# A two-hop graph attention kernel on one core: a drain behind every single matmul and transpose of TensorE in both hops, in place of one behind each group

## What is computed

```python
def _agg(ent, rel, head, tail, etype, fc_w, fc_b):
    a_input = concatenate([ent[head], ent[tail]], axis=-1)
    e_input = sum((a_input @ fc_w.T + fc_b) * rel[etype], axis=-1)
    e = leaky_relu(e_input, negative_slope=0.2)
    m = segment_max(e, head)
    exp_e = exp(e - m[head])
    alpha = exp_e / segment_sum(exp_e, head)[head]
    return segment_sum(ent[tail] * alpha[:, None], head) + ent
for _ in range(2):
    ent = _agg(ent, rel, head, tail, etype, fc_w, fc_b)
    ent = ent / max(norm(ent), 1e-12)
return layernorm(x + ent)
```

## Time and profile before

| what | value |
|---|---|
| median of three runs | 2866.54 us |
| the profiled execution | 2870.03 us |
| its span, first to last instruction | 2867.7 us |
| mean granted TensorE clock (1 is full) | 0.561 |
| TensorE matmul busy | 1218.3 us (42%) |
| TensorE weight load busy | 818.2 us (29%) |
| VectorE busy | 1848.4 us (64%) |
| ScalarE busy | 866.2 us (30%) |
| GpSimd busy | 1805.7 us (63%) |
| bytes moved by DMA | 255.95 MB |

### The profile page before, as it was taken

How to read it: one execution, slowest core, us unless ns; L and a number is a source line. 1 busy time by engine, 2 the same in 40 slices (tenths; PEclk the granted TensorE clock), 3 DMA queues, 4 the chain that set the end, 5 groups by cost and what they waited for, 6 DMA issues and landing times. The chain is left out here.

```text
span 2867.7 us, 22941 instructions
## 1 busy us (share of the span) xinstructions
PE 1218.3 (42%) x4597; PEld 818.2 (29%) x4597; DVE 1848.4 (64%) x3677; ACT 866.2 (30%) x1585; POOL 1805.7 (63%) x1607
## 2 busy tenths in 40 slices
PE   4688801354423544245433534444344345343300
PEld 4577701122211222123212423232223223222200
DVE  6867864286562865546655559877667667766753
ACT  2232304375453754445631212111111111111111
POOL 1000047377774777757777238877777787777776
PEclk9555555555555555555555556665655555566555
DMA  2333333254432444335433133222222222222210
GB/s 68 89 109 103 104 70 84 52 147 131 126 91 71 130 132 131 86 95 150 122 87 114 51 112 89 82 85 79 61 83 87 72 66 84 86 58 66 60 44 13
DMA packets 91815, 255.95 MB, mean 89 GB/s; under 512 B 31782, under 2 KB 39047, under 8 KB 91771
## 3 DMA queue, kind: packets, MB, share of 16 engines
q1 hardware_dynamic: 41403, 183.66, 20.8%
q0 software_dynamic: 50368, 71.78, 11.4%
HBM read 157.76 MB, written 102.23 MB: 91 GB/s over the span
## 5 line engine op out<-in xcount | busy, mean ns | idle before, releaser
L572 POOL DMA_INDIRECT area<-rows,gi x1176 | 1330.2, 1131 | 487.4 <-issue 367.7
L620 POOL DMA_INDIRECT out<-area,place x392 | 459.3, 1172 | 119.5 <-issue 119.5
L765 PE MATMUL psR<-area,row_t 128*98 128x512 f16 (+1 forms) x896 | 302.7, 504 | 454.3 <-DVE area L1191 335.9
L748 PE MATMUL psR<-area 128*128 128x392 f16 x392 | 198.5, 506 | 445.2 <-issue 406.3
L670 PE MATMUL psP<-V,vT 65*125 65x40 f32 (+1 forms) x1586 | 323.4, 393 | 86.1 <-issue 56.6
L670 PEld LDWEIGHTS psP<-V,vT 65*125 65x125 f32 (+1 forms) x1586 | 316.0, 310 | 104.7 <-issue 62.4
L765 PEld LDWEIGHTS psR<-area,row_t 128*98 128x98 f16 x896 | 141.5, 173 | 610.4 <-DVE area L1191 351.9
L908 ACT ACTIVATE area<-area 128x896 f32<-128x896 f32 x84 | 79.8, 950 | 586.2 <-DVE area L1270 433.6
L872 ACT ACTIVATE area<-iota_h,half_hi 128x392 f16<-128x392 f16 x392 | 238.9, 609 | 16.8 <-issue 15.4
L1269 DVE TENSOR_TENSOR area<-SM,rd 128x896 f32<-128x896 f32 x56 | 93.6, 1671 | 206.6 <-DMA out<-area,place 205.4
L774 PE MATMUL psT<-ones,area 98*128 98x1 f32 x700 | 152.6, 352 | 173.5 <-DVE area L1191 131.1
(11 more groups left out here) (269 smaller groups left out, 2296.4 us busy)
## 6 DMA issues: line engine op xcount, KB each, us to landing
rows<-area SPq DMA_DIRECT2D x50, 787.5 KB
area<-tail_digits SPq DMA_DIRECT2D x28, 896.0 KB
rows<-area SPq DMA_DIRECT2D x28, 735.0 KB
area<-rows SPq DMA_DIRECT2D x28, 735.0 KB
area<-rows SPq DMA_DIRECT2D x25, 787.5 KB
area<-rows,gi POOLq DMA_INDIRECT x1176
head_xs<-area SPq DMA_DIRECT2D x28, 448.0 KB
area<-head_xs SPq DMA_DIRECT2D x28, 448.0 KB
```

The source lines that it names most:

```text
L572: pool.indirect_dma_start(out=to[:, b, k, 0:tab.shape[1]], out_offset=None, in_=tab, in_offset=bass.IndirectOffsetOnAxis(ap=gi[:, b, n, k: ...
L620: pool.indirect_dma_start(out=out, out_offset=bass.IndirectOffsetOnAxis(ap=place[:, b, k:k + 1].bitcast(U32), axis=0), in_=rowO[:, b, k, 0 ...
L748: te.matmul(psC, sign_lo[:, (s0 + k) % KS, :], sign_hi[:, (s0 + k) % KS, :], start=static and t0 + k == 0, stop=True, skip_group_check=True)
L765: te.matmul(psR[g % 2][0:HH, 0:w], row_t[:, n, c, :], hot_lo[:, c, 4 * g * P:4 * g * P + w], start=c == 0 and n == 0, stop=c == HB - 1 and ...
```

## The change

A drain stands behind every transpose in `transposes`, every matmul in `products` when it is called from `project`, and every matmul of both kinds in `look`; only the last one of a group carries the increment. `products` of the nodes, ahead of the hops, keeps one drain (`single=False`). In `count` the drain was already behind each matmul; there only the way in which the increment is written changes. In the built program of before the increments were already part of the drains (in the body of the first loop of TensorE there are 42 drains and 4 separate semaphore instructions); in the changed one that body has 88 drains for its 88 matmuls and transposes, and the same 4.

```diff
@@ transposes
                     for k in range(t, min(t + KT, n)):
                         te.transpose(psT[0:w, t // KT, (k - t) * P:(k - t) * P + parts], row(k),
-                                            ident[0:parts, 0:parts])
-                    pe.drain()
-                    pe.sem_inc(tr, 1)
+                                     ident[0:parts, 0:parts])
+                        last = pe.drain()
+                    last.then_inc(tr, 1)
-            def products(n, parts, w, pr):
+            def products(n, parts, w, pr, single=True):
                 half = -(-n // 2)
                 for k in range(n):
                     te.matmul(psP[0:parts, k // half, (k % half) * w:(k % half + 1) * w],
-                                     vT[:, k * P:k * P + parts], V[:, 0:w], start=True, stop=True)
-                pe.drain()
-                pe.sem_inc(pr, 1)
+                              vT[:, k * P:k * P + parts], V[:, 0:w], start=True, stop=True)
+                    if single or k == n - 1:
+                        last = pe.drain()
+                last.then_inc(pr, 1)
@@ node_products
-                products(KN, PN, 2 * R, s_npr)
+                products(KN, PN, 2 * R, s_npr, single=False)
@@ count
-                    pe.drain()
-                    pe.sem_inc(s_cnt, 1)
+                    pe.drain().then_inc(s_cnt, 1)
@@ look
                             te.matmul(psR[g % 2][0:HH, 0:w], row_t[:, n, c, :], hot_lo[:, c, 4 * g * P:4 * g * P + w],
                                              start=c == 0 and n == 0, stop=c == HB - 1 and n == 1)
-                    pe.drain()
-                    pe.sem_inc(s_look, 1)
+                            last = pe.drain()
+                    last.then_inc(s_look, 1)
...
                 for k in range(K):
                     te.matmul(sums[:, k:k + 1], chosen[0:HH, k * P:(k + 1) * P], ones[0:HH, 0:1], start=True, stop=True)
-                pe.drain()
-                pe.sem_inc(s_sum, 1)
+                    last = pe.drain()
+                last.then_inc(s_sum, 1)
```

## The result

Four executions of the changed kernel took 3015.66 to 3046.08 us, median 3029.66; the kernel before beside it 2869.96 us (median of four). The ratio is 1.0555, 95% interval 1.0493 to 1.0618. The forecast was 2990 us (2915 to 3075). The profiled execution took 3033.28 us, its span 3031.0, against 2870.03 and 2867.7: 163.3 us more span.

The account below looks back on a forecast made before the run. GpSimd was taken to bound both hops, with TensorE nearly the chain in the passage between them. Added to the profiled 2870.03 us, 70 (passage) + 48 (first hop's slow stretches) + 2 (second hop) = 120 us gave 2990 us, range 2915 to 3075.

Parts of the forecast that it names:

- The sum of 120 us: Whole kernel: 70 us between the hops, 48 in the first hop, 2 in the second, giving 2990 us; chance 52%.
- The price of one: On TensorE, a drained matmul costs its columns and 0.39 us, taken from the sign matmuls' 0.72 us pitch.
- The passage, +70: Between the hops, TensorE is nearly the chain: 60.85 us become 130.4, 70 us more, with ends of 54 and 80.
- The first hop in its normal course, hidden: First hop: TensorE's chunk grows from 22.6 to 33.0 us, still under GpSimd's 40.3, so nothing is paid.
- The slow stretches of the first hop, +48: Four times in the first hop each instruction is slow; added drains cost 12 us each time, 48 us (0 to 92).
- The second hop, hidden: +2: Second hop: TensorE's chunk of 38.0 us stays under GpSimd's 41.7; only the smaller lead at its start costs 2 us.
- Only the passage pays: Rival, 21%: the first hop's slow stretches last no longer, only the piece between the hops costs: +72, 2942 us.
- The second hop becomes TensorE's: Rival, 14%: drains add 7.4 us to each second-hop chunk, TensorE needs 45.4 us against 41.7: 92 us, 3082 in all.
- Faster: Rival, 7%: drains prevent long bursts, so first-hop waits mostly go: 90 us gained against 72 paid, 2852 us.
- No difference: Rival, 6%: drains cost nothing where TensorE has idle time, or are not carried out singly: 2870 us.
- What would show it: Signs in the changed profile: pitches 0.82, 0.66, 0.86 us; L601 near 150 us; L1143 up some 40; L1269 smaller.

Follow-up runs that it names:

- e5_passage_only: Single drains only in projections 24 to 27, looks 0 to 2 and the seam's, against the kernel before: 2970.66 us beside 2925.87, ratio 1.0197.
- r3_after_third: The unaltered changed kernel run a third time, against the kernel before on another chip without slow stretches: 2822.73 us beside 2766.49, ratio 1.0186.
- e9_inc_third: The changed kernel with its 1792 added drains replaced by increments of an unread semaphore, against the kernel before: 2895.73 us beside 2871.14, ratio 1.0139.

## Why the prediction was right, and where its steps were not

- **The sum of 120 us** stands against 163 measured, inside the range. Its passage was named rightly, its second hop wasn't. That it came out inside owes something to luck: the passage was 13 us too large, the second hop 83 too small, GpSimd's busy time fell by 23 us of which the sum says nothing, and the first hop's size came out right for a wrong reason. It also took a chip with slow stretches; on one without them the same change costs 56 us.
- **The price of one** was put too high. Measured in the changed kernel: transposes 7.63/14 = 0.55 us (0.66 forecast), fp32 products 10.10/14 = 0.72 (0.86), 512 columns 11.75/16 = 0.73 (0.82), 256 columns 0.52 (0.61), sums 0.65 (0.83). The row that I took it from, the sign matmul at 0.72 us, has something in its 0.21 us that the others have not: in the trace, though not in the timeline view, a register instruction of the ring starts 0.084 us ahead of its weights (900.709 and 900.793, behind the stretch of the earlier trace rows). Without it 392 columns cost 0.635 us, and 120 more 0.1: 0.735, as measured. The price of a drained f16 matmul above its columns is 0.31 us, not 0.39. The estimate by the Trainium skill ("TensorE: Matmul & The Clock Gate", section "Single matmul latency") had 0.18 beyond the columns; the runs lie between it and my row, nearer to the row.
- **The passage, +70**: right in place and mechanism, too large. A look and a projection take 50.4 us, not 59.1; the passage 111.0 us, not 130.4. GpSimd's wait at L601 grew by 56.7 us here and, alone, by 55.5 us on a chip without slow stretches (by 70 in `e5_passage_only`, with a stretch over look 0). The range's lower end of 54 was nearer than the value. The assumption of the lower clock held (0.50).
- **The first hop in its normal course, hidden**: confirmed. Without slow stretches the changed kernel has one wait for L1143, of 23.6 us, as the others have. So one of the six waits that the prediction gave to the stretches is there without them, 23.6 us of its 119.7.
- **The slow stretches of the first hop, +48**: measured +46.8 at L1143. The size is right, and in part by luck: on the second chip with slow stretches it was +106 (268.8 against 163.0), and the kernel before alone differs by 43 us between its two traces. The reason that I gave, a price for each instruction, falls. The doubled drains leave the pitch at 2.81 us, with 2.64 us in the first drain and 0.013 in the second, and 1792 increments bring some 40 us (15 to 65) where the drains brought 160 on a like chip. What is paid for in a stretch is the drain's wait behind each row, not the instruction.
- **The second hop, hidden: +2**: this is the step that failed on the first chip: 85.2 us at L1145 against the 2 of the sum. Its undisturbed part was right, with more room than I had: a look of 33.45 us beside 41.7, and looks 3 to 27 drained singly cost nothing (0.9987). I had read the slow stretches as the first hop's matter, since in the trace of before they show in the second hop only as drains a few microseconds late behind bursts. With a drain behind each matmul the same conditions cost each row up to 2.8 us, a look's sums 20.65 us (2480.08 to 2500.73) in place of 9.14 and the gap behind, and GpSimd waits for its indices. The runs show this from both sides: with the hop's drains and no stretches it costs nothing (0.9987 and `r3_after_third`), with stretches and no added drains in the hop it costs nothing either (`e5_passage_only`) or little (one wait of 15.7 us in `e9_inc_third`), and with both together the waits at L1145 come to 85 and 141 us.
- **The rivals.** *Only the passage pays* (21%, 2942 us, +72) is what happens on a chip without slow stretches, with +56. *The second hop becomes TensorE's* named the place of the miss and not its way: not 7.4 us on each chunk, but six waits of GpSimd, of 8 to 26 us. *Faster* was right in one half: no drain ends tens of microseconds late any more, the longest in the hops lasts 6.35 us where it was 58.43. But the stretches stayed, and their cost went into each row; taking the drains away altogether is what gives a gain (36 us). *No difference* is excluded by all three intervals of the changed kernel.
- **What would show it**: L601 near 150 (140.1) and L1143 up by some 40 (46.8) came; pitches of 0.82, 0.66 and 0.86 did not. L1269 smaller came (19.8), yet not for the reason in mind: it kept its 202.5 us where the second hop was hidden.

Open is what makes the slow stretches, whether TensorE's rows really last longer in them or only their ends are told late, and why they come on some chips and not on others (each group was run at one time, so chip and time are not told apart). All runs, timed ones too, had their rows recorded; whether the stretches belong to the recording wasn't tried.

## What to carry to other kernels

A drain behind a matmul costs the wait for that matmul to run empty, here 0.31 us beyond the columns of an f16 matmul at the lower clock, and little for its own sake (0.08 us for a second one). Undisturbed, it is free where TensorE has slack and paid for where TensorE is the chain: look for the passages between phases, not at the mean busy share. An increment on the last matmul itself tells the end of a group without a drain, and was the faster form here in both conditions (by 10 and 36 us).

When a price is taken from a neighbouring row, look at what else stands in its pitch. And when a trace shows a disturbance in one phase, ask what it would cost the other phases once the change has taken their bursts away.

## What the runs showed that was not expected

- The kernel before took 2766 to 2926 us (medians) in five groups of runs; the traces differ by slow stretches. In them singly drained matmul rows stand up to 2.8 us apart, and a drain ends 45 to 55 us late behind one burst of 28 rows, though the rows themselves issue at full pace.
- The granted clock of the changed kernel is 0.50 in each slice of both hops, 0.517 in the mean; with increments in the drains' place it is 0.62 in the passage and 0.60 in the second hop. Singly drained matmuls never got the upper level, with TensorE's rows busy for 95 of 111 us in the passage; back-to-back ones did (there 55 of 74 us busy).
